# Taking |x| of softplus from ScalarE's activation to a bit mask on VectorE, and SyncE's load places from tables, in a Mamba layer with a quantised feed-forward

## Chip, cores, metric

One core of a Trainium2 chip runs the whole program. The metric is the device time of one execution in microseconds.

## What is computed

A Mamba block on a residual stream of 2 x 4096 tokens by 512, a layer norm, a feed-forward layer with weights rounded to -1, 0 or 1, and a second layer norm. The part that matters here:

```
dt = softplus(x_dbl[..., :64] @ dt_proj_w.T + dt_proj_b)        # 1024 channels
h[t] = exp(dt[t] * A) * h[t-1] + dt[t] * B[t] * x[t]              # 16 states a channel
y[t] = sum over the 16 states of h[t] * C[t]
y = (y + x * D) * silu(z);  out = y @ out_proj_w.T
```

Softplus is made as max(x, 0) + log(1 + exp(-|x|)), with a correction for the rounding of 1 + e.

## The kernel before

The Mamba part walks 16 chunks of 512 tokens (`TC`). A chunk has 64 units (`UNITS`): unit u is channel pair q = u // 16 (two blocks of 128 channels) and state n = u % 16. Each unit is a small pipeline:

- SyncE (`load_bb`, L368) brings one row of B, broadcast to 128 partitions, into a ring of four (`bb`).
- GpSimd saves the state of unit u-2 (`save_state`, L563) and makes `dbu` = `dtx` times `bb` (L592).
- ScalarE makes two `decay` tiles in PSUM (L639).
- VectorE runs two scans (L898) into one of three `h` buffers.
- TensorE transposes h (L1192, tile `ht`). ScalarE (L653) or, for twelve units, VectorE (L919) scales by C, and TensorE adds the result into y (L1197).

Everything else of the layer is placed between the units by tables written by hand, one queue for each engine, all in program order. Chunk c carries the input projection, convolution, x projection and the first half of softplus (pairs q = 0 and 1) of the next chunk f, and the output projection and norm of the one before, p. Pairs q = 2 and 3 of softplus for chunk c run at its own beginning. The first chunk's pairs 0 and 1 are made in a prologue. A loop of seven rounds with two chunks each holds chunks 1 to 14.

Softplus of a pair q is a chain across three engines, on tiles of 128x1024:

1. ScalarE takes `dt` from PSUM for each block (`take_dt`, L683, places `TAKE_DT`).
2. ScalarE: `soft` = |dt| (L690), then `soft` = exp(-soft) (L692), in places `EXP_AT`: pairs 2 and 3 in units 3 and 5, pairs 0 and 1 of f in units 48 and 50.
3. VectorE: `rounded` (L872), `dt` = max(dt, 0) + soft (L878, the lift), in places `ROUND_AT` and `LIFT_AT`; these come after the scans of units 5 and 7, and 50 and 52.
4. ScalarE: the logarithm (L698); GpSimd: the excess (L531); VectorE: the sum (L884).
5. GpSimd: `dtx` = dt times x (L539), in places `DTX_AT`.

VectorE's places count three for a unit: 3u comes ahead of its first scan, 3u+1 between the two scans, 3u+2 after both. ScalarE's and TensorE's places count two for a unit.

The weights of the input projection pass through two slots (`win`), one block of 128 columns at a time: z0, x0 to x7, z1 to z7 in a chunk. SyncE loads a block (L366) once the block before it in the same slot has been used (`wait_full`). SyncE has one queue, and a wait in it holds up the `bb` loads behind it.

Of the kernel before, what the change touches and what calls it, by code (L numbers as in the profile page):

```python
# [18 lines left out]
NB = DI // P  # L19
KM = DM // P  # L20
# [47 lines left out]
UNITS = (NB // 2) * NS  # L68
# [66 lines left out]

def banks():

    order = []
    for at in sorted(SLOTS):
        for kind, i, _ in SLOTS[at]:  # L140
            if (kind, i) not in order:
                order.append((kind, i))
    return {name: n % 2 for n, name in enumerate(order)}


BANK = banks()


# [13 lines left out]
def layer(nc, x_tm, x_cm, w_in, conv_w, conv_b, w_xp, w_dt, b_dt, a_log, d_skip, w_out, b_rows, x1, w1, b1, w2, b2, out):  # L162

    ctx = ExitStack()
    with ctx:
# [90 lines left out]
        alog_in = sem("alog_in")  # L256
        win_in = {kind: [sem(f"win_{kind}{i}") for i in range(2)] for kind in "xz"}
        xt_in = sem("xt_in")
# [99 lines left out]
        def _(sp):  # L358
# [3 lines left out]

            def load_win(kind, i):
                block_of = i + (NB if kind == "z" else 0)
                slot = (i + 1) % 2 if kind == "x" else i % 2
                sp.dma_start(win[:, slot, :, :], w_in[block_of]).then_inc(win_in[kind][i % 2], 16)  # L366

# [64 lines left out]
            for i in range(2, NB):  # L432
                wait_full(sp, "x", first, i - 2)
                load_win("x", i)
            store_b(first)

            def chunk(c, is_first, is_last):
# [4 lines left out]

                for u in range(UNITS):
                    if u == 0:
                        if is_first:
                            wait_full(sp, "x", c, NB - 1)
                        else:
                            wait_full(sp, "z", p, NB - 1)
                        load_win("z", 0)
                        if not is_last:  # L450
                            load_win("x", 0)
                        wait(sp, b_out, c, 16, 16)
                    load_bb(c, u)
                    if u == 2 and not is_last:
                        load_xt(f, tok_f)
                    if u == 4 and not is_first:
                        load_x(p, tok_p)
                    if u == 9 and not is_last:
                        wait_full(sp, "z", c, 0)
                        load_win("x", 1)  # L460
                    for i in range(2, NB):
                        if u == 22 + 2 * i and not is_last:
                            wait_full(sp, "x", f, i - 2)
                            load_win("x", i)
                    for i, at in ((1, 38), (2, 40), (3, 42), (4, 44), (5, 50), (6, 58), (7, 60)):
                        if u == at:
                            if i >= 3:
                                wait_full(sp, "z", c, i - 2)
                            elif not is_last:
                                wait_full(sp, "x", f, NB - 3 + i)  # L470
                            elif i == 2:
                                wait_full(sp, "z", c, 0)
                            load_win("z", i)
                    if u == 49 and not is_last:
# [149 lines left out]
        def _(act):  # L624
# [215 lines left out]
        def _(dve):  # L840
# [18 lines left out]
            def conv_save(f, i):  # L859
# [271 lines left out]
        def _(pe):  # L1131
            pe.wait_ge(ident_set, 1)

            def in_proj(kind, chunk, i, parts, room):
                slot = (i + 1) % 2 if kind == "x" else i % 2
                if 0 in parts:
                    room(kind, chunk, i)
                    if i == 0:
                        wait(pe, xt_in, chunk, 16, 16)
                    wait(pe, win_in[kind][i % 2], chunk, NB // 2 * 16, (i // 2 + 1) * 16)  # L1140
                for k in parts:
# [87 lines left out]

            def last_z(p):  # L1230

                held = [None, None]
                for i in (NB - 2, NB - 1):
                    held[BANK["z", i]] = ("z", p, i)
                return held
# [3 lines left out]
            for i in range(NB):  # L1239
                in_proj("x", first, i, range(KM), room)  # L1240
            pe.wait_ge(weights_in, 16 * N_WEIGHTS)
# [5 lines left out]
            def chunk(c, is_first, is_last):  # L1247
                p, f = c.near(-1), c.near(1)
                room = prologue if is_first else rooms(last_z(p))

                def slot(at):
                    for kind, i, parts in SLOTS.get(at, ()):
                        if kind == "z":
                            in_proj("z", c, i, parts, room)
                        elif kind == "o":
                            if not is_first:
                                out_proj(p, i, parts, room)
                        elif not is_last:
                            if kind == "x":
                                in_proj("x", f, i, parts, room)  # L1260
                            elif kind == "xd":
# [131 lines left out]
```

## Time and profile before

| | us |
|---|---|
| median of 3 runs | 5187.58 |
| the runs | 5177.46 to 5194.58 |
| the profiled execution | 5189.64 |
| its span in the profile | 5187.8 |
| TensorE busy | 4515.9 (87% of the span) |
| VectorE busy | 4051.2 (78%) |
| ScalarE busy | 3573.7 (69%) |
| GpSimd busy | 3165.4 (61%) |

Read the shares with care: they are means over the Mamba part, which takes about the first 4150 us, and the feed-forward part behind it, in which GpSimd does nothing and TensorE is busy nearly all the time.

### The profile page before, as it was taken

The numbers are of one execution on the slowest core, as the hardware profiler recorded it, in microseconds if no ns is written. First come the engines' busy times: TensorE is split into PE (matmuls) and PEld (weight loads), VectorE is DVE, ScalarE is ACT, GpSimd is POOL, SyncE is SP. The second block draws the span as 40 slices with busy tenths as digits, with TensorE's granted clock in tenths as the row PEclk, the third lists the DMA queues.
The fourth block names the chain that finished last, engine by engine and source line by source line (L and its number), as shares of the span: only waits on it lengthen the run. The fifth ranks groups of instructions, "written<-read, shape, count | busy, mean of one in ns | idle before, by whom it ended". The sixth has DMA issues, their size and how long they took to land.

```text
span 5187.8 us, 85358 instructions
## 1 busy us (share of the span) xinstructions
PE 4515.9 (87%) x23362; PEld 3155.1 (61%) x23362; DVE 4051.2 (78%) x4782; ACT 3573.7 (69%) x6726; POOL 3165.4 (61%) x2471
## 2 busy tenths in 40 slices
PE   5979897989797989897989898888888799999998
PEld 3656565656565656555655555555555568888887
DVE  5888888888888888888888888888888864444454
ACT  5888887878787878787878787878787722222222
POOL 4787868686868686868686868686868600000000
PEclk8999998989999989898989898999998899999999
DMA  3323323332323233333333333232324300110000
GB/s 95 97 89 96 98 93 97 92 100 91 100 90 100 93 99 90 98 90 98 90 98 91 98 91 99 92 102 89 100 90 148 109 17 33 37 43 32 32 32 33
DMA packets 233374, 436.69 MB, mean 84 GB/s; under 512 B 23968, under 2 KB 24096, under 8 KB 232416
## 3 DMA queue, kind: packets, MB, share of 16 engines
q1 hardware_dynamic: 232928, 431.55, 27.0%
q8 instruction: 181, 2.97, 0.2%
q14 instruction: 265, 2.17, 0.1%
HBM read 397.38 MB, written 34.08 MB: 83 GB/s over the span
## 4 chain that ended last, share of the span: by engine, by line
PE 58%; ACT 13%; DVE 13%; issue 10%; POOL 4%; DVEq 1%; ACTq 1%; DMA 0%; POOLq 0%; SPq 0%
PE gemm L1142 13%; PE ht L1192 12%; PE y L1197 9%; PE ht L1319 8%; DVE h L898 7%; PE gemm L1176 5%; ACT ch L653 5%; PE y L1332 4%; PE gemm L1332 4%; ACT decay L639 4%; POOL dbu L592 2%; PE gemm L1152 2%; POOL x L526 1%; ACT dt L683 1%; ACT soft L690 1%
## 5 line engine op out<-in xcount | busy, mean ns | idle before, releaser
L898 DVE TENSOR_TENSOR_SCAN h<-decay,carry,dbu 128x512 f32<-128x512 f32 x2048 | 2522.8, 1269 | 296.0 <-ACT decay L639 178.9
L592 POOL TENSOR_TENSOR dbu<-dtx,bb 128x1024 f32<-128x1024 f32 x1024 | 2458.2, 2401 | 5.6 <-issue 2.4
L639 ACT ACTIVATE decay<-dt,aneg 128x512 f32<-128x512 f32 x2048 | 1429.3, 700 | 689.0 <-DVE h L898 684.7
L1192 PE MATMUL ht<-ident,h 128*128 128x128 f32 x8192 | 1342.5, 292 | 620.5 <-DVE h L898 458.6
L1192 PEld LDWEIGHTS ht<-ident,h 128*128 128x128 f32 x8192 | 1018.6, 149 | 1335.6 <-issue 830.3
L653 ACT ACTIVATE ch<-ht,ct 128x256 f32<-128x256 f32 x3328 | 1401.3, 481 | 110.8 <-PE ht L1192 108.2
L1142 PE MATMUL gemm<-xt,win 128*128 128x512 f32 x2048 | 1063.3, 604 | 11.0 <-DMA win<-w_in 7.2
L1197 PEld LDWEIGHTS y<-ident,ch 128*128 128x128 f32 x6656 | 795.3, 144 | 404.1 <-issue 363.8
L1197 PE MATMUL y<-ident,ch 128*128 128x128 f32 x6656 | 898.5, 279 | 4.2 <-DVE x L925 2.6
L566 POOL TENSOR_TENSOR carry<-h,ones_pair 128x2 f32<-128x2 f32 x1022 | 271.4, 266 | 870.3 <-DVE h L898 860.1
L818 ACT ACTIVATE hr<-ht,b1c 128x512 f32<-128x512 f32 x256 | 176.4, 689 | 707.9 <-PE ht L1319 707.9
L1176 PE MATMUL gemm<-wout,x 128*128 128x512 f32 x1024 | 532.4, 607 | 0.0
L1099 DVE CAST hhi<-hr 128x512 fp32r<-128x512 f32 x256 | 109.4, 427 | 461.6 <-ACT hr L818 461.5
L1319 PE MATMUL ht<-xhi,wq 128*128 128x512 f32 x1024 | 398.9, 390 | 0.8 <-DVE xres L932 0.8
L1319 PE MATMUL ht<-xlo,wq 128*128 128x512 f32 x1024 | 398.8, 389 | 0.0
L1142 PEld LDWEIGHTS gemm<-xt,win 128*128 128x128 f32 x2048 | 317.3, 194 | 28.2 <-issue 20.9
L919 DVE SCALAR_TENSOR_TENSOR ya<-ht,ct,ya 128x256 f32<-128x256 f32 x512 | 221.3, 477 | 116.8 <-PE ht L1192 116.3
L855 DVE SCALAR_TENSOR_TENSOR x<-gemm,cw,x 128x511 f32<-128x511 f32 (+2 forms) x384 | 281.3, 733 | 20.6 <-ACT x L661 15.8
L1319 PEld LDWEIGHTS ht<-xhi,wq 128*128 128x128 f32 x1024 | 192.3, 188 | 42.8 <-DVE xres L932 1.6
L1319 PEld LDWEIGHTS ht<-xlo,wq 128*128 128x128 f32 x1024 | 192.2, 188 | 40.4
L1332 PE MATMUL y<-wq,hhi 128*128 128x512 f32 x512 | 204.7, 400 | 4.0 <-DVE hlo L1101 3.8
L1332 PE MATMUL gemm<-wq,hhi 128*128 128x512 f32 x512 | 200.5, 392 | 0.0
(91 smaller groups left out, 3974.8 us busy)
## 6 DMA issues: line engine op xcount, KB each, us to landing
bb<-b_rows SPq DMA_DIRECT2D x1024, 256.0 KB, 3.3
win<-w_in SPq DMA_DIRECT2D x256, 256.0 KB, 3.7
xt<-x_cm SPq DMA_DIRECT2D x16, 1024.0 KB, 6.8
xres<-x_tm SPq DMA_DIRECT2D x16, 1024.0 KB, 6.9
x<-xres SPq DMA_DIRECT2D x16, 1024.0 KB, 5.1
xr<-x SPq DMA_DIRECT2D x16, 1024.0 KB, 5.4
out<-xr SPq DMA_DIRECT2D x16, 1024.0 KB, 4.3
raw<-w SPq DMA_DIRECT2D x8, 1024.0 KB, 7.5
```

Source lines behind the costliest of these rows:

```text
L566: nc.gpsimd.tensor_tensor(carry[:, c.par, n, pair(q)], h[:, H_SLOT[u], :, TC - 1], ones[:, :], ALU.mult)\
L592: nc.gpsimd.tensor_tensor(dbu[:, u % 2, :, :], dtx[:, pair(q), :], bb[:, u % BB_RING:u % BB_RING + 1, :].to_broadcast([P, 2, TC]), ALU.mul ...
L639: nc.scalar.activation(DA[j][:, :], dt[:, c.par, i, :], ACT.Exp, scale=aneg[:, i, n:n + 1])\
L653: ins = nc.scalar.activation(ch[:, b % 2, tb, :], HT[k][:, tb % 2, :], ACT.Copy, scale=ct[:, c.par, tb, n:n + 1])
L855: nc.vector.scalar_tensor_tensor(x[:, f.par, i, back:], G[BANK["x", i]][:, 0:TC - back], cw[:, i, KC - 1 - back:KC - back], x[:, f.par, i, ...
L898: nc.vector.tensor_tensor_scan(h[:, H_SLOT[u], j, :], DA[j][:, :], dbu[:, u % 2, j, :], carry[:, c.par, n, i:i + 1], ALU.mult, ALU.add).th ...
L1142: ins = nc.tensor.matmul(G[BANK[kind, i]][:, :], win[:, slot, k, :], xt[:, chunk.par, k, :], start=(k == 0), stop=(k == KM - 1))
L1176: ins = nc.tensor.matmul(G[BANK["o", tb]][:, :], x[:, p.par, i, tb * P:(tb + 1) * P], wout[:, i, :], start=(i == 0), stop=(i == NB - 1))
L1192: ins = nc.tensor.transpose(HT[k][:, tb % 2, j * P:(j + 1) * P], h[:, H_SLOT[u], j, tb * P:(tb + 1) * P], ident[:, :])
L1197: return nc.tensor.matmul(Y[j][:, tb * P:(tb + 1) * P], src, ident[:, :], start=begins and tb == 0, stop=False, is_transpose=True, skip_gr ...
L1319: ins = nc.tensor.matmul(HP[j % 2][:, :], w1q[k][:, j * P:(j + 1) * P], part[:, k, :], start=(k == 0 and part is xhi), stop=(k == KM - 1 a ...
L1332: ins = nc.tensor.matmul(OP[tb][:, :], part[:, j % 2, tb * P:(tb + 1) * P], w2q[j // KM][:, j % KM, :], start=(j == 0 and part is hhi), st ...
```

## The change

The ScalarE activation Abs is gone. VectorE masks the sign bit instead, in places of its own: pair 2 ahead of the scans of unit 4, pair 3 ahead of those of unit 6, pair 0 of f after the scans of unit 49, and pair 1 of f between the two scans of unit 51. ScalarE's exp waits for it. Its own places are unchanged.

SyncE's loads of `win` have their places from a table: a block is loaded five units after the unit in which the block before it in its slot is last used. Places go from 26, 28, ... 36 to 24, 26, ... 34 for x2 to x7; from 38, 40, 42, 44, 50, 58, 60 to 36, 38, 40, 42, 48, 56, 58 for z1 to z7; and from 9 to 6 for x1. In a unit they now stand ahead of that unit's `bb` load and no longer behind it. The slots have one semaphore each, and TensorE's waits count on these.

```
+ABS_AT = {12: 2, 18: 3, 149: 0, 154: 1}
+XT_AT, X_AT, B_AT = 2, 4, 49
+LOAD_LAG = 5
+def loads(order):
+    at = {}
+    for n in range(len(order)):
+        if n < 2:
+            u = 0
+        else:
+            last = max(slot for slot in SLOTS for kind, i, _ in SLOTS[slot] if (kind, i) == order[n - 2])
+            u = min(last // 2 + LOAD_LAG, UNITS - 1)
+        at.setdefault(u, []).append(n)
+    return at
...
+            def load_next_win(c, order, n):
+                user = order[n - 2] if n >= 2 else WIN_ORDER[n - 2]
+                owner = c if n >= 2 else c.near(-1)
+                wait_full(sp, user[0], owner.near(1) if user[0] == "x" else owner, user[1])
+                load_win(n % 2, order[n][0], order[n][1])
...
                 for u in range(UNITS):
+                    order, at = (WIN_LAST, WIN_LAST_AT) if is_last else (WIN_ORDER, WIN_AT)
+                    for n in at.get(u, ()):
+                        if is_first and n < 2:
+                            wait_full(sp, "x", c, NB - 2 + n)
+                            load_win(n, order[n][0], order[n][1])
+                        else:
+                            load_next_win(c, order, n)
...
                     load_bb(c, u)
...
             def softplus_exp(f, q):
-                wait(act, dt_ready, f, NP, q - 1)
-                wait_read(act, "dt", f, 2 * q + 1)
-                nc.scalar.activation(soft[:, q % 2, :, :], dt[:, f.par, pair(q), :], ACT.Abs).then_inc(abs_ready, 1)
                 wait(act, abs_ready, f, NP, q + 1)
                 nc.scalar.activation(soft[:, q % 2, :, :], soft[:, q % 2, :, :], ACT.Exp, scale=-1.0).then_inc(e_ready, 1)
...
+            def softplus_abs(f, q):
+                wait(dve, dt_ready, f, NP, q - 1)
+                wait_read(dve, "dt", f, 2 * q + 1)
+                nc.vector.tensor_scalar(soft[:, q % 2, :, :].bitcast(U32), dt[:, f.par, pair(q), :].bitcast(U32), 0x7FFFFFFF,
+                                        None, ALU.bitwise_and)\
+                    .then_inc(abs_ready, 1)
...
+            for q in (0, 1):
+                softplus_abs(first, q)
...
+                    if at in ABS_AT:
+                        if ABS_AT[at] >= 2:
+                            softplus_abs(c, ABS_AT[at])
+                        elif not is_last:
+                            softplus_abs(f, ABS_AT[at])
                     for q in ROUND_AT.get(at, ()):
```

## Rows read from the trace of the kernel before

**Rows 1.** The page's chain that ended last, by engine and by line.

```profile
PE 58%; ACT 13%; DVE 13%; issue 10%; POOL 4%; DVEq 1%; ACTq 1%; DMA 0%; POOLq 0%; SPq 0%
PE gemm L1142 13%; PE ht L1192 12%; PE y L1197 9%; PE ht L1319 8%; DVE h L898 7%; PE gemm L1176 5%; ACT ch L653 5%; PE y L1332 4%; PE gemm L1332 4%; ACT decay L639 4%; POOL dbu L592 2%; PE gemm L1152 2%; POOL x L526 1%; ACT dt L683 1%; ACT soft L690 1%
```

**Rows 2.** All instructions of one line: ns as min/median/max, first and last start.

```profile
L690 ACT ACTIVATE soft<-dt x64: 1040/1094/1195, 64.0 to 3937.8; 128x1024 f32<-128x1024 f32 x64
...
L872 DVE TENSOR_SCALAR rounded<-soft x64: 667/894/2253, 67.5 to 3943.1; 128x1024 f32<-128x1024 f32 x64
```

**Rows 3.** Timeline, ScalarE, units 48 to 51: start, length, instruction, idle before.

```profile
1535.29 1.19 ACT L690 ACTIVATE soft<-dt 128x1024 f32<-128x1024 f32 x1
1536.51 1.06 ACT L692 ACTIVATE soft<-soft 128x1024 f32<-128x1024 f32 x1
...
1545.06 1.12 ACT L690 ACTIVATE soft<-dt 128x1024 f32<-128x1024 f32 x1
1546.21 1.06 ACT L692 ACTIVATE soft<-soft 128x1024 f32<-128x1024 f32 x1
```

**Rows 4.** Timeline, VectorE, the scans of units 49, 50 and 51.

```profile
1532.41 2.53 DVE L898 TENSOR_TENSOR_SCAN h<-decay,carry,dbu 128x512 f32<-128x512 f32 x2 [1.31 <-ACT decay L639]
1538.28 2.52 DVE L898 TENSOR_TENSOR_SCAN h<-decay,carry,dbu 128x512 f32<-128x512 f32 x2 [3.34 <-ACT decay L639]
...
1545.02 2.44 DVE L898 TENSOR_TENSOR_SCAN h<-decay,carry,dbu 128x512 f32<-128x512 f32 x2
```

**Rows 5.** Timeline, VectorE and then GpSimd, units 3 to 7 of a chunk.

```profile
1610.63 2.45 DVE L898 TENSOR_TENSOR_SCAN h<-decay,carry,dbu 128x512 f32<-128x512 f32 x2
...
1621.50 1.67 DVE L872 TENSOR_SCALAR rounded<-soft 128x1024 f32<-128x1024 f32 x1
1623.09 3.53 DVE L878 SCALAR_TENSOR_TENSOR dt<-dt,soft 128x1024 f32<-128x1024 f32 x1
1626.54 3.62 DVE L898 TENSOR_TENSOR_SCAN h<-decay,carry,dbu 128x512 f32<-128x512 f32 x3
...
1612.83 2.36 POOL L592 TENSOR_TENSOR dbu<-dtx,bb 128x1024 f32<-128x1024 f32 x1
...
1621.32 1.27 POOL L539 TENSOR_TENSOR dtx<-dt,x 128x512 f32<-128x512 f32 x1
...
1623.18 2.36 POOL L592 TENSOR_TENSOR dbu<-dtx,bb 128x1024 f32<-128x1024 f32 x1
```

**Rows 6.** Timeline, pair 2's Abs and sum in this chunk and the next.

```profile
1616.18 1.08 ACT L690 ACTIVATE soft<-dt 128x1024 f32<-128x1024 f32 x1
...
1653.85 3.15 DVE L884 SCALAR_TENSOR_TENSOR dt<-soft,dt 128x1024 f32<-128x1024 f32 x1
...
1877.72 1.08 ACT L690 ACTIVATE soft<-dt 128x1024 f32<-128x1024 f32 x1
...
1884.51 1.21 DVE L878 SCALAR_TENSOR_TENSOR dt<-dt,soft 128x1024 f32<-128x1024 f32 x1
1885.64 3.63 DVE L898 TENSOR_TENSOR_SCAN h<-decay,carry,dbu 128x512 f32<-128x512 f32 x3
...
1911.60 3.14 DVE L884 SCALAR_TENSOR_TENSOR dt<-soft,dt 128x1024 f32<-128x1024 f32 x1
```

**Rows 7.** Group of the lift: busy us, mean ns of one, idle us before.

```profile
L878 DVE SCALAR_TENSOR_TENSOR dt<-dt,soft 128x1024 f32<-128x1024 f32 x64 | 91.6, 1431 | 0.0
```

**Rows 8.** Busy time by stretch: PE, PEld, DVE, ACT, POOL, then granted clock, DMA.

```profile
1629.30:1632.70 3.40, 3.35 (x10) 2.21 (x11) 3.40 (x4) 3.26 (x7) 3.40 (x3) 0.50 0.03 8
```

**Rows 9.** `win` and `bb`: group, z3's last matmuls, unit 48's dbu, landing of `bb`.

```profile
L1142 PE MATMUL gemm<-xt,win 128*128 128x512 f32 x2048 | 1063.3, 604 | 11.0 <-DMA win<-w_in 7.2 <-DVE hist L863 3.8
...
1776.60 1.02 PE L1142 MATMUL gemm<-xt,win 128*128 128x512 f32 x2
...
1782.04 2.36 POOL L592 TENSOR_TENSOR dbu<-dtx,bb 128x1024 f32<-128x1024 f32 x1
...
DMA to landing us min/median/max: 3.0/3.3/7.8
```

More of the change, by code:

```diff
@@ L140, in banks @@
         for kind, i, _ in SLOTS[at]:
-            if (kind, i) not in order:
+            if kind in kinds and (kind, i) not in order:
                 order.append((kind, i))
-    return {name: n % 2 for n, name in enumerate(order)}
+    return order
+def banks():
+    return {name: n % 2 for n, name in enumerate(begun(KINDS))}
+def loads(order):
[8 more added lines that the diff above has]
+    return at
 BANK = banks()
+WIN_ORDER = begun("xz")
+WIN_LAST = begun("z")
+WIN_AT, WIN_LAST_AT = loads(WIN_ORDER), loads(WIN_LAST)
 STATS_AFTER = {1: (0, 1), 2: (2, 3)}
@@ L256, in layer @@
         alog_in = sem("alog_in")
-        win_in = {kind: [sem(f"win_{kind}{i}") for i in range(2)] for kind in "xz"}
+        win_in = [sem(f"win_in{i}") for i in range(2)]
         xt_in = sem("xt_in")
@@ L443, in chunk @@
                 for u in range(UNITS):
-                    if u == 0:
[L445 to L451, printed above, removed]
+                    order, at = (WIN_LAST, WIN_LAST_AT) if is_last else (WIN_ORDER, WIN_AT)
[5 more added lines that the diff above has]
+                            load_next_win(c, order, n)
+                    if u == 0:
                         wait(sp, b_out, c, 16, 16)
                     load_bb(c, u)
-                    if u == 2 and not is_last:
+                    if u == XT_AT and not is_last:
+                        wait_full(sp, "z", p, NB - 1)
                         load_xt(f, tok_f)
-                    if u == 4 and not is_first:
+                    if u == X_AT and not is_first:
                         load_x(p, tok_p)
[L458 to L474, printed above, removed]
+                    if u == B_AT and not is_last:
                         store_b(f)
@@ L1132, in _, with in_proj @@
             pe.wait_ge(ident_set, 1)
-            def in_proj(kind, chunk, i, parts, room):
-                slot = (i + 1) % 2 if kind == "x" else i % 2
+            def in_proj(kind, chunk, i, parts, room, n, earlier=NB // 2):
+                slot = n % 2
                 if 0 in parts:
@@ L1139, in in_proj @@
                         wait(pe, xt_in, chunk, 16, 16)
-                    wait(pe, win_in[kind][i % 2], chunk, NB // 2 * 16, (i // 2 + 1) * 16)
+                    wait(pe, win_in[slot], chunk if kind == "z" else chunk.near(-1), NB * 16, (earlier + n // 2 + 1) * 16)
                 for k in parts:
@@ L1228, in rooms, with held_after, held_at_end @@
                 return room
-            def last_z(p):
+            def held_after(p):
+                order = begun(KINDS)
                 held = [None, None]
-                for i in (NB - 2, NB - 1):
-                    held[BANK["z", i]] = ("z", p, i)
+                for kind, i in order[-2:]:
+                    held[BANK[kind, i]] = (kind, p if kind in "zo" else p.near(1), i)
+                return held
+            def held_at_end(last):
+                held = [None, None]
+                for kind, i in begun("zo"):
+                    held[BANK[kind, i]] = (kind, last if kind == "z" else last.near(-1), i)
                 return held
@@ L1239, in _ @@
             for i in range(NB):
-                in_proj("x", first, i, range(KM), room)
+                in_proj("x", first, i, range(KM), room, i, NB)
             pe.wait_ge(weights_in, 16 * N_WEIGHTS)
@@ L1248, in chunk @@
                 p, f = c.near(-1), c.near(1)
-                room = prologue if is_first else rooms(last_z(p))
+                room = prologue if is_first else rooms(held_after(p))
                 def slot(at):
@@ L1253, in slot @@
                         if kind == "z":
-                            in_proj("z", c, i, parts, room)
+                            n = (WIN_LAST if is_last else WIN_ORDER).index((kind, i))
+                            in_proj("z", c, i, parts, room, n)
                         elif kind == "o":
@@ L1259, in slot @@
                             if kind == "x":
-                                in_proj("x", f, i, parts, room)
+                                in_proj("x", f, i, parts, room, WIN_ORDER.index((kind, i)))
                             elif kind == "xd":
@@ L1289, in _ @@
             sum_over_n(last, UNITS - 1)
-            room = rooms(last_z(last))
+            room = rooms(held_at_end(last))
             room("o", last, 1)
@@ L1297, in _ @@
             transpose_rows(0, 0, 0, range(2))
-            room = rooms(last_z(last))
+            room = rooms(held_at_end(last))
             for tb in range(TB):
```

15 lines of the change are left out of this document (7 added, 8 removed).

## The prediction

> **What bounds the kernel now.** I read the chain that ended last first. TensorE holds 58% of it, ScalarE and VectorE 13% each, GpSimd 4% [rows 1]. No engine is the bound throughout: the chain changes hands inside each chunk. Abs itself (L690) has 1% of the chain, about 50 us, and its 64 instructions are only 64 x 1.09 = 70 us [rows 1, 2]. So most of Abs lies on the path today, and the question is what takes its place. For that I read the timeline at the two stretches in which it runs.
>
> Units 48 to 51 belong to ScalarE. VectorE waits 1.31 and 3.34 us for the decays of units 49 and 50 [rows 4], while ScalarE goes without a gap through dt, Abs and exp [rows 3].
>
> Units 3 to 7 belong to VectorE and GpSimd together. Each hinders the other there. The rounding of pair 2 takes 1.67 us where its fastest copy takes 0.67 [rows 5, 2]. It starts at 1621.50, GpSimd's dtx runs from 1621.32 to 1622.59, and 1622.59 + 0.6 is where the rounding ends. The lift behind it takes 3.53 us: GpSimd's dbu of unit 7 runs from 1623.18 to 1625.54, and 1.1 us later the lift is done [rows 5]. One chunk later the same lift takes 1.21 [rows 6]. So these VectorE instructions and GpSimd's exclude each other, and it is an open race which goes first. Over all 64 lifts the mean is 1.43 [rows 7], so (1.43 - 1.21) x 64 / (3.53 - 1.21) = 6 are long ones: of the 15 chunks after the first, six lose this race and nine win it. A lost race costs more than itself. From Abs of pair 2 to its sum a chunk that loses takes 1653.85 - 1616.18 = 37.7 us, one that wins 1911.60 - 1877.72 = 33.9 [rows 6]. The first scan of unit 6 is later by (1626.54 - 1616.18) - (1885.64 - 1877.72) = 2.4 us. The remaining 1.4 us is TensorE: it waits for those scans, and the stretch after it runs at a granted clock of 0.50, the lower level of 1.2 GHz [rows 8].
>
> The Trainium skill says the same of the two engines (SBUF — State Buffer, Who interferes with whom): a VectorE instruction with two SBUF inputs, or a one-input one that uses both ports, and a GpSimd instruction lock each other out for whole instructions. The trace agrees with its 1.67 and 3.53 us. The term below would be the same without this sentence.
>
> **The new instruction.** The trace has no bitwise mask. The nearest row is the rounding: also one input, one constant, 128x1024, SBUF to SBUF, 0.67 us when free [rows 2]. Slowest I allow the free lift's 1.21 us, at one element a step [rows 6]. I take 0.6 us of exclusive use, since the new instruction differs from the rounding only in operation and type.
>
> **Pairs 0 and 1 of the next chunk (15 times).** Pair 0: ScalarE is free at about 1535.3, where Abs starts today [rows 3]. VectorE ends unit 49's scans at 1532.41 + 2.53 = 1534.94 and then waits 3.34 us, so the mask fits in and ends at about 1535.6. With a wait of 0.15 the exp starts at 1535.75 instead of 1536.51 [rows 3, 4]: 0.75 us gained, up to 1.1 at best. GpSimd is held up by 0.6 at most and its next dbu is not wanted for 6 us.
> Pair 1: the mask stands after the first scan of unit 51. This starts at 1545.02, now 0.75 earlier, and ends 1.25 later at 1545.5. The mask ends at 1546.15 and exp starts at 1546.3. Before it started at 1546.21, which sounds like a draw; in the other form of this stretch, where the rounding ahead is 2.25 us (the longest of its rows [rows 2]) in place of 1.95, it comes 0.3 later, at 1546.6. Behind that exp stand the decay and the C scaling of the next units, for which TensorE waits. So pair 1 gives back all that pair 0 gained, and a little more: +0.35 us on this path, with ends of -0.75 (everything gained is kept) and +1.2 (a mask of 1.21 us). 15 x 0.35 = **+5 us**.
>
> **Pairs 2 and 3 (15 like these, and the first chunk).** Pair 2's mask is issued when unit 3's scans end, 1610.63 + 2.45 = 1613.08. GpSimd's dbu of unit 4 has the ports from 1612.83 to 1615.19 [rows 5]. The mask runs from 1615.2 to 1615.8. ScalarE gains 1.08 us on its exp, but nobody needs it: GpSimd, busy without a gap from here to 1625.5, is now 0.6 late with dtx and the dbu of units 5 and 6, and scans of unit 5 end at about 1622.0 instead of 1621.6.
> Then VectorE has rounding, lift and now the mask of pair 3 ahead of unit 6's scan; GpSimd has dtx, the saved state and unit 7's dbu. In the likelier orders one dtx (1.27) and one dbu (2.36) come ahead of the mask: even if the lift wins against the dbu, the dbu has been waiting and goes ahead of the mask. Counting from dbu of unit 6, which ends at 1621.95: 1.25 + 0.6 + 2.36 + 1.1 + 0.6 gives 1627.9 for unit 6's first scan. Before it was 1626.54 in a losing chunk, and 1624.1 would be the winning one. If the mask slips in ahead of the dbu, it is 1625.6.
> In time: a losing chunk gets 1.35 longer, a winning one 3.8 + 1.35 = 5.1. All bad: 6 x 1.35 + 9 x 5.1 = 54 us. All good: 1.5 more than a winning chunk, with part of TensorE's loss 1.8; 9 x 1.8 - 6 x (3.8 - 1.8) = +4 us. I take two chunks in three for the bad order: 0.67 x 54 + 0.33 x 4 = **+37 us**.
> ScalarE's exp of pair 3 must now wait for the mask, from 1624.7 to about 1628. Queued behind it is the decay of unit 7, but this needs the scan of unit 6 anyway.
>
> **Prologue.** VectorE is idle there, and two Abs of 1.04 us [rows 2] leave a bare chain: **-2 us**.
>
> **Load places.** Today `win` costs TensorE 7.2 us in one wait, at the very start, over 2048 matmuls [rows 9]. Earlier loads can't gain more than nothing. What they can lose: a `win` load waits for TensorE, and now `bb` loads stand behind it. The tightest place is unit 48. Its `bb` now waits until z3 has been used, 1776.60 + 1.02 = 1777.6. With one `win` issue of about 0.4 us ahead it lands 3.3 us later at 1781.4, and unit 48's dbu is to start at 1782.04 [rows 9]. If two transfers at a time slow it, by 1 us say, the dbu is 0.4 late; VectorE's 1.31 us wait for ScalarE in unit 49 covers that [rows 4]. So **0**; uncovered at the slowest landing, 7.8 us, it is 7.8 - 3.3 - 0.65 - 1.3 = 2.5 us in each such chunk. x1 to x7 have more room, as their units come later than TensorE's use. The lists of x_t and of the stored B keep their units.
>
> **Sum.** 5 + 37 - 2 = +40 us on the profiled execution: 5189.6 + 40 = 5229.6. This execution lies 2.1 above the median of the runs shown, so 5228.
>
> **The rivals.**
> - *ScalarE sets the pace (faster).* If the masks of pairs 1 and 3 were ready when ScalarE arrives, as pair 0's nearly is, the path would shrink by Abs itself. For: Abs has 1% of the chain. Against: pair 3's mask stands behind the rounding and lift of pair 2, and ScalarE comes to its exp two us before them. All four would give 15 x 4.4 = 66 us, two of four, pairs 0 and 2, 15 x (0.75 + 1.08) = 27 us, so 5160. It decides where the mask is done before ScalarE's dt is. The Trainium skill (ScalarE: Activation LUTs, Rules for kernel authors) would send simple functions to VectorE for speed alone; by the two shortest rows that is 1.04 against 0.67, and it does not count the queue. Chance 0.17.
> - *The race falls well (no change).* Shifting GpSimd by 0.6 us makes VectorE win everywhere: +4 + 5 - 2, so 5195; with pair 1 at its good end, 5185. Chance 0.13.
> - *The `bb` loads come late.* The wait at unit 48 is not covered: up to 15 x 1.5 = 22 us on top, 5250. For: 0.65 us of room. Against: the cover in unit 49. Chance 0.07.
> - *The mask goes at one element a cycle and locks nobody out.* Then pair 2 is free, pair 3 adds 1.2 x 1.3 in each chunk and pair 1 adds 1.2: 15 x 2.7 - 2 = +39. Another mechanism, same time; it is part of my forecast's 0.63.
>
> **How the numbers follow.** A measurement of this kernel tells about 0.3% (15 us) from no change. My forecast, 0.63, and late `bb`, 0.07, are slower: 0.70. Same 0.13, faster 0.17. The range goes down to 5172, which takes in the well-falling race and half of the faster case, and up to 5262, all chunks bad with 1.2 us for each pair 1. Left out are about 2 in 10.
>
> **What would show it.** Mask: L-group of 128x1024 at 0.67 us when free, with about 2.7 us for pair 2. ScalarE idle ahead of exp: about 1.5 to 2 us for pair 1, 2 to 3 for pair 3, released by VectorE. From unit 3 to the sum of pair 2: 39 us in most chunks. More stretches at half clock behind unit 6. `bb` at unit 48 landing within 1 us of its dbu. I am wrong if the mask of pair 3 goes ahead of dbu in most chunks, or if the pattern of the race elsewhere, which I did not follow past unit 13, changes with the new phase.

## The result and the profile after

| | before | after |
|---|---|---|
| median of the timed runs, us | 5189.04 (12 runs) | 5206.1 (12 runs, 5196.45 to 5212.76) |
| ratio | 1 | 1.0035, 95% interval 1.0024 to 1.0045 |
| profiled run / its span, us | 5189.6 / 5187.8 | 5212.76 / 5211.0 |

The change costs 17 us. It is slower, as forecast, but by less than half of the 40 us.

In the chain that ended last of the kernel after, ScalarE has 9% where it had 13%, VectorE 15% where it had 13%, and the issue share grew from 10% to 12% [rows 1]. Abs has left the chain; VectorE has taken part of its place.

```profile
PE 56%; DVE 15%; issue 12%; ACT 9%; POOL 5%; DVEq 1%; ACTq 0%; POOLq 0%; DMA 0%; SPq 0%
PE gemm L1171 12%; PE ht L1221 12%; DVE h L920 8%; PE y L1226 8%; PE ht L1357 8%; PE gemm L1205 5%; PE y L1370 4%; PE gemm L1370 4%; ACT ch L670 3%; ACT decay L656 3%; POOL dbu L609 3%; PE gemm L1181 2%; POOL x L543 2%; DVEq L54 1%; DVE dt L900 1%
```

All instructions of the mask's line in the kernel after, ns as min/median/max, first and last start:

```profile
L883 DVE TENSOR_SCALAR soft<-dt x64: 659/675/2980, 60.7 to 3958.0; 128x1024 uint32<-128x1024 uint32 x64
```

Its groups of the lift and of dbu, busy us, mean ns, idle us before and what ended it:

```profile
L900 DVE SCALAR_TENSOR_TENSOR dt<-dt,soft 128x1024 f32<-128x1024 f32 x64 | 90.7, 1418 | 0.0
...
L609 POOL TENSOR_TENSOR dbu<-dtx,bb 128x1024 f32<-128x1024 f32 x1024 | 2459.3, 2402 | 9.8 <-DMA bb<-b_rows 4.6
```

A free mask takes 0.66 to 0.68 us, which is the rounding's time [rows 2]. Its longest is 2.98, so it does exclude GpSimd, and GpSimd it.

Units 3 to 6 of one chunk in the timeline, VectorE and then GpSimd. This answers to [rows 5]:

```profile
859.28 2.66 DVE L883 TENSOR_SCALAR soft<-dt 128x1024 uint32<-128x1024 uint32 x1
...
865.57 2.46 DVE L920 TENSOR_TENSOR_SCAN h<-decay,carry,dbu 128x512 f32<-128x512 f32 x2 [1.27 <-POOL dbu L609]
867.95 0.67 DVE L894 TENSOR_SCALAR rounded<-soft 128x1024 f32<-128x1024 f32 x1
868.53 2.30 DVE L900 SCALAR_TENSOR_TENSOR dt<-dt,soft 128x1024 f32<-128x1024 f32 x1
870.75 0.68 DVE L883 TENSOR_SCALAR soft<-dt 128x1024 uint32<-128x1024 uint32 x1
871.36 2.45 DVE L920 TENSOR_TENSOR_SCAN h<-decay,carry,dbu 128x512 f32<-128x512 f32 x2
...
867.98 1.77 POOL L556 TENSOR_TENSOR dtx<-dt,x 128x512 f32<-128x512 f32 x1
869.72 1.17 POOL L583 TENSOR_TENSOR carry<-h,ones_pair 128x2 f32<-128x2 f32 x1
870.84 2.82 POOL L609 TENSOR_TENSOR dbu<-dtx,bb 128x1024 f32<-128x1024 f32 x1
```

Read it as a row of handovers. The rounding starts 0.03 us ahead of dtx and runs free, in 0.67. dtx waits for it (1.77 where 1.27 is its free time) and the lift waits for dtx (2.30 for 1.21). GpSimd's small copy of the state (`carry`, 0.19 when free) then waits for the lift, and while it does, the dbu behind it is not yet there to claim the ports. So the mask of pair 3 goes first, in 0.68, and the dbu waits. By "the ports" I mean, as in the prediction, what these two engines cannot use at once. In 12 of the 15 chunks ahead of the last the mask of pair 3 is free like this (14 in after_again, 13 in mask_only and in mask_pairs23). In the other three, the first among them, and in the last chunk it is blocked, as here:

```profile
1634.93 1.84 DVE L894 TENSOR_SCALAR rounded<-soft 128x1024 f32<-128x1024 f32 x1
1636.69 1.21 DVE L900 SCALAR_TENSOR_TENSOR dt<-dt,soft 128x1024 f32<-128x1024 f32 x1
1637.83 2.84 DVE L883 TENSOR_SCALAR soft<-dt 128x1024 uint32<-128x1024 uint32 x1
...
1636.17 0.65 POOL L583 TENSOR_TENSOR carry<-h,ones_pair 128x2 f32<-128x2 f32 x1
1636.78 3.33 POOL L609 TENSOR_TENSOR dbu<-dtx,bb 128x1024 f32<-128x1024 f32 x1
```

Here dtx won. The copy of the state is over as the lift begins (1636.82), the dbu queues up during the lift (1636.78), and the mask has to let it pass.

Units 49 to 51 of the kernel after, VectorE and then ScalarE, for [rows 3, 4]:

```profile
1289.41 0.67 DVE L883 TENSOR_SCALAR soft<-dt 128x1024 uint32<-128x1024 uint32 x1
1291.88 2.53 DVE L920 TENSOR_TENSOR_SCAN h<-decay,carry,dbu 128x512 f32<-128x512 f32 x2 [1.80 <-ACT decay L656]
...
1290.11 1.06 ACT L706 ACTIVATE soft<-soft 128x1024 f32<-128x1024 f32 x1
...
1300.81 1.06 ACT L706 ACTIVATE soft<-soft 128x1024 f32<-128x1024 f32 x1 [1.97 <-DVE soft L883]
```

VectorE's wait ahead of unit 50 fell from 3.34 to 1.80 us, and ScalarE now waits 1.97 us for pair 1's mask.

For the comparison by place I add up, over the 15 chunks ahead of the last, the time between the first scans of named units, as they stand in VectorE's timelines. Three profiles have Abs on ScalarE (before, before_again, loads_only), three have all four masks (after, after_again, mask_only):

| units | Abs on ScalarE | all four masks | mean difference |
|---|---|---|---|
| 0 to 3 | 157.6, 158.8, 159.7 | 162.7, 161.7, 159.1 | +2.5 |
| 3 to 6 | 216.0, 211.9, 216.6 | 222.6, 220.8, 223.4 | +7.4 |
| 6 to 13 | 437.5, 434.9, 437.5 | 433.7, 431.3, 431.4 | -4.5 |
| 13 to 40 | 1534.7, 1535.9, 1535.5 | 1535.7, 1535.6, 1535.2 | +0.1 |
| 40 to 52 | 673.0, 673.6, 673.5 | 673.4, 671.5, 672.5 | -0.9 |
| 55 to 60 | 281.3, 283.2, 282.8 | 289.2, 290.2, 289.0 | +7.0 |
| last chunk, 3 to 6 | 13.5, 13.5, 13.5 | 16.9, 16.8, 16.9 | +3.4 |

The places that I had priced are 3 to 13 and 48 to 52. Units 6 to 13 got shorter because the long lifts are gone: in the kernel before they took 30.4 us in four of the six chunks that lost the race and 29.0 or 29.1 in the others behind the first; in the kernel after 29.0, and 31.3 once. Units 55 to 60 are as dear as 3 to 6, and I had no term for them. What happens there shows in one chunk of each kernel: the window, then VectorE's two rows in it, of before and of after.

```profile
1565.01:1571.81 6.80, 3.95 (x18) 2.29 (x19) 6.53 (x9) 3.31 (x6) 5.47 (x4) 1.00 0.20 70
```

```profile
1568.47 0.88 DVE L919 SCALAR_TENSOR_TENSOR ya<-ht,ct,ya 128x256 f32<-128x256 f32 x2 [0.27 <-PE ht L1192]
1569.26 1.27 DVE L898 TENSOR_TENSOR_SCAN h<-decay,carry,dbu 128x512 f32<-128x512 f32 x1
```

```profile
1577.02:1583.82 6.80, 5.38 (x12) 2.67 (x12) 4.92 (x8) 2.07 (x3) 4.83 (x3) 0.51 0.17 39
```

```profile
1582.20 0.88 DVE L941 SCALAR_TENSOR_TENSOR ya<-ht,ct,ya 128x256 f32<-128x256 f32 x2 [1.68 <-PE ht L1221]
1583.00 1.27 DVE L920 TENSOR_TENSOR_SCAN h<-decay,carry,dbu 128x512 f32<-128x512 f32 x1
```

The columns of a window are busy time and instructions of PE, PEld, DVE, ACT and POOL, then granted clock, DMA share and GB/s. TensorE's 18 matmuls of the first window take 0.22 us on average, the 12 of the second 0.45. At the same place after unit 54's first scan the granted clock is 1.00 in the one and 0.51 in the other, 2.4 GHz and 1.2. In the second TensorE's transposes come later, VectorE's product with C waits 1.68 us for them instead of 0.27, and so the second scan of unit 56 starts 1.7 us later. By the start of unit 57 1.1 us of it is left. In all six profiles this holds chunk by chunk: behind the first chunk, unit 57 starts 17.7 us after unit 54 where the clock is full in this stretch and 18.8 where it is halved throughout; most chunks lie between, in clock and in time. Full were 8, 4 and 5 of the 15 chunks with Abs on ScalarE, and 1, 0 and 0 with the masks.

### The profile page after: what moved, and what is told of

It is laid out like the page before. It is cut to its first block, busy times and chain, and to the rows that moved or that the text cites. A ratio compares the mean times of both kernels' runs of the same rounds, so it can differ in the third digit from the quotient of the medians.

```text
span 5211.0 us, 85386 instructions
## 1 busy us (share of the span) xinstructions
PE 4538.0 (87%) x23362; PEld 3163.9 (61%) x23362; DVE 4106.5 (79%) x4846; ACT 3515.1 (67%) x6662; POOL 3189.4 (61%) x2471
## 4 chain that ended last, share of the span: by engine, by line
PE 56%; DVE 15%; issue 12%; ACT 9%; POOL 5%; DVEq 1%; ACTq 0%; POOLq 0%; DMA 0%; SPq 0%
PE gemm L1171 12%; PE ht L1221 12%; DVE h L920 8%; PE y L1226 8%; PE ht L1357 8%; PE gemm L1205 5%; PE y L1370 4%; PE gemm L1370 4%; ACT ch L670 3%; ACT decay L656 3%; POOL dbu L609 3%; PE gemm L1181 2%; POOL x L543 2%; DVEq L54 1%; DVE dt L900 1%
## 5 line engine op out<-in xcount | busy, mean ns | idle before, releaser
L1171 PE MATMUL gemm<-xt,win 128*128 128x512 f32 x2048 | 1077.1, 611 | 11.9 <-DMA win<-w_in 7.3
L583 POOL TENSOR_TENSOR carry<-h,ones_pair 128x2 f32<-128x2 f32 x1022 | 282.9, 277 | 857.7 <-DVE h L920 847.1
```

What stands on the lines that cost most here:

```text
L583: nc.gpsimd.tensor_tensor(carry[:, c.par, n, pair(q)], h[:, H_SLOT[u], :, TC - 1], ones[:, :], ALU.mult)\
L1171: ins = nc.tensor.matmul(G[BANK[kind, i]][:, :], win[:, slot, k, :], xt[:, chunk.par, k, :], start=(k == 0), stop=(k == KM - 1))
```

## The experiments

Their times stand beside those of the kernel before on the same chip. loads_only, mask_only, mask_pairs01 and mask_pairs23 shared one chip (before 5188.24 us); mask_pair2, mask_pair3, after_dtx8 and mask01_early another (5194.31); mask23_at12, mask012, mask012_early and before_again a third (5188.98); mask_pair2_again, mask02 and after_again a fourth (5183.67).

**Only one half of the change.** loads_only: the new load tables, Abs left on ScalarE. mask_only: the masks, the old load places.

```
 # loads_only, softplus_exp
+                wait(act, dt_ready, f, NP, q - 1)
+                wait_read(act, "dt", f, 2 * q + 1)
+                nc.scalar.activation(soft[...], dt[...], ACT.Abs).then_inc(abs_ready, 1)
```

> The changed kernel with Abs back on ScalarE, so only the load places differ from the kernel before. Theory A: within 3 us of the kernel before. Theory B: +12 to +17 us, with GpSimd waiting for bb at unit 48. Theory C: no loss in units 3 to 13 or 40 to 52, but a different count of half-clock stretches in units 0 to 3 and 55 to 60, and up to 10 us either way.

> The kernel before with the mask on VectorE in its four places, SyncE's loads as before. Theory A (the mask, by its place ahead of the scans of unit 6 and by the shared lock, makes the loss): the whole loss stays, +15 to +20 us against the kernel before. Theory B (the load places make it, by bb loads held up at unit 48 and by win loads at other times): 0 to +5 us. Theory C (the loss is in stretches at half clock that any small shift of the chunks moves about): a result between -10 and +20 us that does not add up with the loads-only kernel to +17.

loads_only: 5185.94 us, ratio 0.9996 (0.9986 to 1.0006). mask_only: 5205.17, 1.0037 (1.0023 to 1.0052). The whole loss is the mask's; the load places cost nothing. In the kernel after GpSimd did wait for `bb`, 4.6 us in seven waits (group of dbu above), 1.0 at most; by these two runs it costs nothing.

**Half of the pairs.** mask_pairs01 masks pairs 0 and 1 on VectorE and leaves Abs of 2 and 3 on ScalarE; mask_pairs23 is the reverse.

```
-ABS_AT = {12: 2, 18: 3, 149: 0, 154: 1}
+ABS_AT = {149: 0, 154: 1}     # mask_pairs01; mask_pairs23: {12: 2, 18: 3}
```

> The changed kernel with pairs 2 and 3 back on ScalarE's Abs; pairs 0 and 1 are masked on VectorE in places 149 and 154. From the profile of the changed kernel these two come out even (ScalarE wins 0.9 us at the exp of pair 0 and waits 1.97 us for the mask of pair 1). Theory A: 0 +- 4 us against the kernel before, since pairs 2 and 3 carry the loss. Theory C: the units 40 to 52 even, and the total wherever the half-clock stretches fall.

> The changed kernel with pairs 0 and 1 back on ScalarE's Abs; pairs 2 and 3 are masked in places 12 and 18. Theory A: +13 to +20 us, all of the loss. The stretch of units 3 to 6 should take 14.4 us in most chunks, as in the changed kernel, and 17 in those where dbu goes ahead. Theory C: units 3 to 13 give no more than +3 us over all chunks, and the rest of any loss lies in units 0 to 3 and 55 to 60.

mask_pairs01: 5190.21 us, 1.0004 (0.9994 to 1.0014). mask_pairs23: 5206.67, 1.0039 (1.0026 to 1.0053), 18 us. The loss lies with pairs 2 and 3. But it does not lie at one place. Against the mean of the three profiles with Abs on ScalarE, mask_pairs23 takes 4.4 us more in units 3 to 6, 4.2 less in 6 to 13, 3.4 more in the last chunk's 3 to 6, 1.6 more in 55 to 60, and 8.4 more in units 0 to 3, where the kernel after has only 2.5.

**Pair 2 alone and pair 3 alone.**

```
-ABS_AT = {12: 2, 18: 3, 149: 0, 154: 1}
+ABS_AT = {12: 2}              # mask_pair2; mask_pair3: {18: 3}
```

> The changed kernel with only pair 2 masked on VectorE (place 12); the other three on ScalarE. Theory A1 (the 0.6 us of pair 3's mask, in VectorE's queue ahead of unit 6's scans, is the loss): within 4 us of the kernel before; units 3 to 6 take 13.5 or less in most chunks. Theory A2 (pair 2's mask waits 2 us for GpSimd and then holds GpSimd up by 0.6 us, in a stretch where GpSimd has no gap): +5 to +12 us, and units 3 to 6 take 14 us.

> The changed kernel with only pair 3 masked on VectorE (place 18). Theory A1: +10 to +17 us, units 3 to 6 at 14 to 14.5 us in chunks where 13.5 was the short form. Theory A2: +3 to +8 us. If neither alone costs more than 5 us, it is the two together that do.

mask_pair2: 5171.43 us, 0.9954 (0.9941 to 0.9967), 23 us faster (12 in the repeat on another chip, below). mask_pair3: 5228.26, 1.0066 (1.0053 to 1.0079), 34 us slower. Of one instruction, at two places of one stretch, one gains and the other loses. Units 3 to 6 add up to 206.9 and 245.4 us, where 212 to 217 is usual. Units 0 to 3 move too, without a mask in them: 150.0 and 141.7 us for 157.6 to 159.7. So the loss of pair 3's mask in units 3 to 13, 35 us, is larger than what the whole profiled execution lost (5219.79 us, the fastest of five, 25 over before). Pair 3 alone, VectorE and then GpSimd:

```profile
867.86 1.56 DVE L898 TENSOR_SCALAR rounded<-soft 128x1024 f32<-128x1024 f32 x1
869.33 1.21 DVE L904 SCALAR_TENSOR_TENSOR dt<-dt,soft 128x1024 f32<-128x1024 f32 x1
870.47 2.84 DVE L887 TENSOR_SCALAR soft<-dt 128x1024 uint32<-128x1024 uint32 x1
873.23 1.27 DVE L924 TENSOR_TENSOR_SCAN h<-decay,carry,dbu 128x512 f32<-128x512 f32 x1
...
867.57 1.28 POOL L556 TENSOR_TENSOR dtx<-dt,x 128x512 f32<-128x512 f32 x1
...
869.42 3.34 POOL L609 TENSOR_TENSOR dbu<-dtx,bb 128x1024 f32<-128x1024 f32 x1
```

This is the order that I had forecast: dtx first, then the dbu that has waited through the lift, then the mask. Unit 3 to unit 6 takes 16.2 us where a winning chunk of before takes 13.5, in 7 of the 15 chunks; seven more take 16.5 to 16.8, five of them with the dbu ahead of the lift instead. Pair 2 alone (VectorE, then ScalarE's Abs of pair 3):

```profile
855.84 0.67 DVE L898 TENSOR_SCALAR rounded<-soft 128x1024 f32<-128x1024 f32 x1
856.42 2.30 DVE L904 SCALAR_TENSOR_TENSOR dt<-dt,soft 128x1024 f32<-128x1024 f32 x1
858.64 3.76 DVE L924 TENSOR_TENSOR_SCAN h<-decay,carry,dbu 128x512 f32<-128x512 f32 x3
...
857.45 1.07 ACT L708 ACTIVATE soft<-dt 128x1024 f32<-128x1024 f32 x1
```

Pair 2's mask holds dtx back: it now starts 11.05 us after unit 3's first scan instead of 10.6, and the rounding at 11.0 instead of 10.9. So the rounding wins in 13 of 15 chunks, the lift takes 2.30 there, and unit 6 comes at 13.8 us after unit 3, 14.3 at most. The margin is thin: the two start within 0.03 us of each other, and in one chunk of mask_pairs23 dtx won from the same start times. The lost races of before, 15.9 to 16.2 us in six chunks, are gone.

**dtx out of the way.** after_dtx8 is the kernel after with dtx of block 3 in unit 8 instead of 6, so that the lift of pair 2 need not wait for it.

```
-DTX_AT = {60: (0,), 61: (1,), 4: (2,), 6: (3,), ...}
+DTX_AT = {60: (0,), 61: (1,), 4: (2,), 8: (3,), ...}
```

> The changed kernel with one more edit: GpSimd makes dtx block 3 in unit 8 and not in unit 6, so that its 1.27 us are no longer between VectorE's rounding and its lift. Lock theory (the two exclude each other): the lift of pair 2 falls from 2.30 to 1.2 us, units 3 to 6 from 14.4 to about 13.2, and the time by 10 to 18 us against the changed kernel, to about 5190. If the lift is 2.3 us for a reason of its own, nothing changes.

5230.92 us, 1.0067 (1.0054 to 1.0080): 37 us slower than before, so about 20 slower than after, where I expected a gain. VectorE and then GpSimd:

```profile
865.47 0.67 DVE L894 TENSOR_SCALAR rounded<-soft 128x1024 f32<-128x1024 f32 x1
866.05 1.22 DVE L900 SCALAR_TENSOR_TENSOR dt<-dt,soft 128x1024 f32<-128x1024 f32 x1
867.18 2.84 DVE L883 TENSOR_SCALAR soft<-dt 128x1024 uint32<-128x1024 uint32 x1
...
875.49 2.29 DVE L900 SCALAR_TENSOR_TENSOR dt<-dt,soft 128x1024 f32<-128x1024 f32 x1
...
866.14 3.34 POOL L609 TENSOR_TENSOR dbu<-dtx,bb 128x1024 f32<-128x1024 f32 x1
...
874.97 1.73 POOL L556 TENSOR_TENSOR dtx<-dt,x 128x512 f32<-128x512 f32 x1
```

The lift fell to 1.22 us, as meant. But without dtx the dbu is there during the lift, and the mask waits for it in all 15 chunks: 15.5 us from unit 3 to unit 6, where after has 14.4. And dtx has met the next lift, of pair 3 (2.29): against the mean of the three profiles with all four masks, units 6 to 13 take 18 us more and units 3 to 6 10 more, while 0 to 3 and 55 to 60 take 14 less. So the run's time is no clean price of the blocked mask, but the order in the rows is: dtx was what kept the dbu away from the mask.

**Pair 3's mask behind pair 2's.** mask23_at12 keeps all four masks and moves pair 3's ahead of the rounding.

```
-ABS_AT = {12: 2, 18: 3, 149: 0, 154: 1}
+ABS_AT = {12: (2, 3), 149: (0,), 154: (1,)}
```

> The kernel after with pair 3's mask moved from place 18 (behind pair 2's lift, ahead of unit 6's scans) to place 12, right behind pair 2's mask; all four masks stay on VectorE. Theory A (pair 3's mask costs by its place: behind the lift it costs 0.67 us where it keeps the shared port and 2.84 where the state update of GpSimd goes ahead): behind pair 2's mask, which has let GpSimd's waiting operation go ahead of it, it costs about 0.67 us, and unit 5's scans and the round start as much later; units 3 to 6 take 13.8 + 0.7 = 14.5 us, as after, but without the 17.0 us chunks; about 0 to -8 us against the kernel after, so 1.002 to 1.0035. Rival B: the second mask in a row waits for GpSimd as pair 1's did at place 150 (2.8 us); then units 3 to 6 take 15.5 to 16 us and the time is about 1.006 to 1.008.

5194.3 us, 1.0005 (0.9994 to 1.0017): no difference from before, where after has 1.0035. VectorE (both masks in one row), then GpSimd:

```profile
853.36 4.35 DVE L883 TENSOR_SCALAR soft<-dt 128x1024 uint32<-128x1024 uint32 x2
...
855.42 1.74 POOL L556 TENSOR_TENSOR dtx<-dt,x 128x512 f32<-128x512 f32 x1
```

The second mask waits, but for the shorter dtx, and takes 1.77 us in most chunks. This delays unit 4 (6.6 us behind unit 3 instead of 4.9), and the next two units follow sooner (2.5 and 5.3 us instead of 3.7 and 5.8), so that the usual chunk takes 14.4 as before the move. What is gone are the chunks of 17: units 3 to 6 sum up to 216.0 us, and the last chunk takes 14.5 instead of 16.9. Both of my prices were off: it is neither 0.67 for the mask nor 2.8. Units 55 to 60 kept their loss (290.1).

**Pair 1 early.** mask01_early has pairs 0 and 1 masked and pair 1's mask right behind pair 0's.

```
-ABS_AT = {12: 2, 18: 3, 149: 0, 154: 1}
+ABS_AT = {149: 0, 150: 1}
```

> Masks for pairs 0 and 1 only, pair 1's moved from place 154 to 150, ahead of the scans of unit 50, where VectorE waits 1.8 us anyway; pairs 2 and 3 on ScalarE. If ScalarE sets the pace in units 48 to 51, as the 1.97 us of its wait for pair 1's mask say, units 48 to 55 get 1.9 us shorter in each of 15 chunks: 28 us, about 5160. If another engine takes over at once (GpSimd or VectorE), half of that or less.

5187.68 us, 0.9982 (0.9971 to 0.9992), 7 us where I had expected 28. VectorE, then GpSimd:

```profile
1031.40 3.57 DVE L887 TENSOR_SCALAR soft<-dt 128x1024 uint32<-128x1024 uint32 x2
1034.90 2.45 DVE L924 TENSOR_TENSOR_SCAN h<-decay,carry,dbu 128x512 f32<-128x512 f32 x2
...
1032.08 2.35 POOL L609 TENSOR_TENSOR dbu<-dtx,bb 128x1024 f32<-128x1024 f32 x1
```

The two masks take 3.57 us, since the dbu goes between them. The scan of unit 50 comes no earlier than before. Units 40 to 52 gain 5 us against before and 52 to 55 3.5, and 55 to 60 lose 3 to 5 again.

**Combinations.** mask012 has pairs 0, 1 and 2 masked (149, 154, 12), mask012_early the same with pair 1 at 150, mask02 pairs 0 and 2 (149, 12). The other pairs have Abs on ScalarE. mask_pair2_again and after_again are repeats, before_again is the kernel before.

> The kernel after with pair 3's absolute value alone back on ScalarE (activation in front of its Exp); pairs 0, 1 and 2 are masked on VectorE at places 149, 154 and 12. Theory A (the loss is pair 3's mask behind pair 2's lift, pair 2's mask gains, and the effects add up): pair 2's mask alone gave 0.9954 and pairs 0 and 1 alone 1.0004, so about 0.9958 of the kernel before, or about -22 us; units 3 to 6 take 13.8 to 13.9 us a chunk where they took 14.4 to 14.6 after. Rival B (the masks cost by their number, 0.67 to 2.8 us each in VectorE's queue, and pair 2's gain was of that run's own): with three of four masks about 1.000 to 1.002.

> As mask012, but pair 1's mask at place 150 in place of 154, right behind pair 0's. Theory A (additive): the early place of pairs 0 and 1 alone gave 0.9982 against 1.0004 for the late one, so about 0.9936, or -33 us, 11 us less than mask012, and 0.8 us less a chunk in units 48 to 52. Rival B: what the early place saves is given back in the units behind, where in the earlier profile 9 of 13 us came back; then the same as mask012 within 5 us.

> The kernel before, unchanged, profiled once more, to see how far one profile differs from another. Theory A (the stretches of units 0 to 3 and 55 to 60, and which chunks have the long lift of pair 2, differ from profile to profile with the granted clock): units 55 to 60 sum up to 1.5 to 5 us more or less than in the first profile over 15 chunks, units 0 to 3 to as much, and another number of chunks than six has units 3 to 6 at 15.9 to 16.2 us. Rival B (the same program always falls the same way): the sums agree within 1 us, and the same six chunks are long.

> Only pair 2 masked on VectorE at place 12, the kernel of mask_pair2 once more. Theory A (its gain is real, and pairs 0 and 1 cost it 10 to 15 us through units 0 to 3, since mask012 was 1.6 us at a per-chunk gain short of it): 0.995 to 0.9965 again, units 0 to 3 near 150 us over 15 chunks where mask012 had 165.6. Rival B (the gain was partly that run's own; the effects do add up): 0.998, as mask012, and units 0 to 3 at 158 to 166 us.

> Pairs 0 and 2 masked on VectorE at places 149 and 12; pairs 1 and 3 have their activation back on ScalarE. Theory A (pair 1's mask at place 154 moves units 0 to 3 and takes pair 2's gain away): as mask_pair2, 0.995 to 0.9965. Rival B (pair 0's mask, which leads unit 50 by 1 us, is the one that moves the later stretches; or the difference lies between runs): 0.998 to 0.999, as mask012.

> The changed kernel, unchanged. Theory A (the loss of 17 us is pair 3's mask in units 3 to 6, about 8 us over the 15 chunks, the last chunk's units 3 to 6, 3 to 4 us, and units 55 to 60, 6 to 8 us, which follow the granted clock at a place that the masks move systematically): about 1.0035 again; the masks of pair 3 take 0.68 us in 11 to 14 of 15 chunks; units 55 to 60 sum up to 287 to 290 us where three profiles of streams as before gave 281 to 283. Rival B (the 8 us of units 55 to 60 were that profile's chance): 281 to 284 us there.

| kernel | us | ratio (95%) | units 48 to 52, sum | units 0 to 3, sum |
|---|---|---|---|---|
| mask012 | 5183.27 | 0.9984 (0.9971 to 0.9996) | 288.1 | 165.6 |
| mask012_early | 5176.69 | 0.9975 (0.9965 to 0.9985) | 282.3 | 162.1 |
| mask_pair2_again | 5172.1 | 0.9985 (0.9976 to 0.9994) | 289.9 | 148.9 |
| mask02 | 5170.96 | 0.9967 (0.9955 to 0.9978) | 274.2 | 161.3 |
| after_again | 5204.64 | 1.0043 (1.0029 to 1.0057) | 287.1 | 161.7 |
| before_again | 5190.95, one run | | 291.1 | 158.8 |

The effects don't add up: pairs 0, 1 and 2 together are 6 us faster than before, not 22. That was not chance. mask_pair2 came out at 5171.4 and 5172.1 on two chips (the ratios differ by 0.3% because before did, 5194 and 5184, so its gain is 12 to 23 us), and its units 0 to 3 sum up to 150.0 and 148.9 us, where the three combinations that also mask pair 0 have 161 to 166. The difference is in a few chunks of 13 us and more in units 0 to 3, where the others take about 9: one in either profile of pair 2 alone, none with pair 3 alone, four or five in the combinations. Counted from 0 they are chunks 3, 7, 9 and 11 in before, before_again, after and mask02 alike, each the first of a round of the loop. In all of these TensorE's weight loads stand still for 4.2 to 5.7 us in units 1 and 2 and wait for nothing that the profile shows; in the other chunks from 1 to 14 such a standstill is 2.0 us at most. The granted clock does not tell them apart: in before, chunk 3 takes 13.9 us at 0.77, chunk 4 takes 9.1 at 0.78. What the standstill is, and why the masks switch it, no run here shows. Before_again shows what one profile hides: four long chunks in units 3 to 6 instead of six, units 55 to 60 1.9 us more.

mask02 separates pair 0 from pair 1. VectorE, then ScalarE:

```profile
1027.02 0.67 DVE L887 TENSOR_SCALAR soft<-dt 128x1024 uint32<-128x1024 uint32 x1
1029.49 2.52 DVE L924 TENSOR_TENSOR_SCAN h<-decay,carry,dbu 128x512 f32<-128x512 f32 x2 [1.80 <-ACT decay L656]
...
1039.18 2.52 DVE L924 TENSOR_TENSOR_SCAN h<-decay,carry,dbu 128x512 f32<-128x512 f32 x2 [0.51 <-ACT decay L656]
...
1036.26 1.13 ACT L708 ACTIVATE soft<-dt 128x1024 f32<-128x1024 f32 x1
1037.42 1.06 ACT L710 ACTIVATE soft<-soft 128x1024 f32<-128x1024 f32 x1
```

From unit 50's first scan to unit 52's it is 9.7 us here. In the kernel after it is 10.7 in this chunk, 10.5 on average: its exp of pair 1 starts 8.9 us behind the scan of unit 50, waiting for VectorE, against 7.9 here, with an Abs in front of it. So pair 0's mask gains 1.1 us a chunk (291 to 274) and pair 1's gives 0.85 back (units 50 to 52, 145.4 to 158.1 us over the 15 chunks). mask02 has the lowest median of all, 13 us under before; pair 2 alone is 1 us away. Four of mask02's twelve executions took 5152 to 5161 us and the others 5168 to 5173, which is not explained. Against pair 2 alone, pair 0's 16 us return as 12 us in units 0 to 3 and 3 in 55 to 60.

## Why the prediction was wrong

**The failed step is the term for pairs 2 and 3: "I take two chunks in three for the bad order", +37 us.** Measured by itself (mask_pairs23) it is +18. At the place that the term is about, it is less still: units 3 to 13 and the last chunk's 3 to 6 add up to 7.4 - 4.5 + 3.4 = +6 us in the kernel after. The chunks fell the other way: the mask of pair 3 went ahead of the dbu in 12 of 15. I had named this myself as what would make me wrong. My prices for one chunk were better than the weight, but too high as well. From unit 3 to unit 6 the good order takes 14.4 us, 0.9 more than a winning chunk of before (I had 1.5), and the bad order 17.0 (I had 17.3). The 1.4 us that a lost race costs behind unit 6 are 0.6 to 0.9 on average in the three profiles with Abs on ScalarE. "All bad", which I had at 54 us, is what mask_pair3 comes nearest to (without pair 2's mask): 35 us in units 3 to 13.

With the weight as it fell, my own prices give 0.2 x 54 + 0.8 x 4 = 14 for this term and 14 + 5 - 2 = 17 in all, which is the measured loss. That would have been luck: 7 of the 17 us lie in units 55 to 60, for which I had no term.

What I missed is the link between my own two steps. I worked out that pair 2's mask makes GpSimd's dtx 0.6 us late, and then took the race behind it as if it were still as open as before. It is hardly open: a dtx 0.45 us later loses to the rounding, if only by a few hundredths of a us, the lift then holds up the state copy, and with it the dbu that would have stood in front of the mask. mask_pair2 (rounding ahead in 13 of 15 chunks) and mask_pair3 (race lost, mask blocked) show both halves, and after_dtx8 shows that dtx is the piece between.

- **The cost of a mask**, 0.6 to 0.67 us of exclusive use and about 2.7 for pair 2's: right (0.67; 2.64 to 2.78 in 11 of 15 chunks, free in three).
- **Pairs 0 and 1, +5 us**: +2 (1.0004), inside the interval. The mechanism holds, one gains what the other gives back: 0.98 us a chunk from unit 49 to 50 (I had 0.75) against 0.85 from 50 to 52 (I had 1.1). The wait of ScalarE for pair 1 was forecast at 1.5 to 2 us and is 1.97; pair 3's, forecast at 2 to 3, is 1.78 in most chunks and 4.03 in a bad one.
- **Load places, 0**: right, 0.9996. The waits for `bb` came, at most 1.0 us, and were covered.
- **Prologue, -2 us**: not to be told. The first scan starts at 83.7 to 87.7 us in the profiles with Abs on ScalarE and at 84.0 to 85.4 with all masks.
- **More half clock behind unit 6**: there the sum even falls by 4.5 us. It came in units 55 to 60, +7 us, in three profiles of three of the masks in their places; that the pattern might change where I did not follow it I had named too. That it goes with the granted clock is shown chunk by chunk; why the masks turn it there is not settled. Masks of 0, 1 and 2 leave it at 285.2, mask_pairs01 has 286.9, mask_pairs23 284.0, and all four with dtx elsewhere (after_dtx8) 284.5. The lowest is mask012_early, 281.3; mask02 has 287.5, and the other kernel with all four, mask23_at12, 290.1.
- **The last chunk**: +3.4 us that I counted as another ordinary one. There dtx goes first and the mask takes 2.98.
- **Two sums were wrong.** The race that falls well with pair 1 at its good end is 4 - 11 - 2, so 5178 and not 5185; all bad with 1.2 us for each pair 1 is 54 + 18 - 2, so 5258 and not 5262. Neither changes the forecast.
- Sum of the means in the table: 2.5 + 7.4 - 4.5 + 0.1 - 0.9 + 7.0 + 3.4 = +15 us, against +17 timed.

Of the rivals, "the race falls well" is the one that took place, with its own price too low (it foresaw 5195): the 0.67 us of pair 3's mask remains on the path, and units 55 to 60 come on top. "ScalarE sets the pace" is true of pair 0, and pair 1 gave it away. It is not true of pair 2: with its mask alone the usual chunk takes 13.8 us from unit 3 to 6, 0.3 more than a winning chunk of before, and the gain comes from the lost races that are gone and from units 0 to 3 (8, 5 and 9 us less in units 3 to 6, 6 to 13 and 0 to 3). I had written 27 us for pairs 0 and 2, and mask02, which is just these two, gains 13.

The Trainium skill (SBUF — State Buffer, Who interferes with whom) says that the order of issue, not the form of the operation, decides who is blocked. The traces agree: the same mask takes 0.67, 1.77 or 2.84 us, by what GpSimd had issued when it arrived.

## What to carry to other kernels

When an operation moves to an engine that shares a port with another, its price is set by what the other engine has waiting when it arrives. Follow each delay that the first moved operation causes into the next race, before giving that race odds. And test moved operations one by one: the four masks here are worth about -16 and +13 us (pairs 0 and 1, by units 48 to 52) and -12 to -23 and +34 us (pairs 2 and 3, each run alone). They do not add up either, since each also moves stretches that hold no mask; only the sum looked like a small loss.

## What the runs showed of the hardware

- A waiting GpSimd instruction takes the ports when VectorE's ends, even if VectorE's next one is ready: mask 2.84 us behind a lift, in mask_pair3 and after_dtx8. VectorE likewise gets its turn after one GpSimd instruction: in mask23_at12 the second mask runs behind dtx (1.77 us), and the copy of the state that GpSimd has ready waits for it (0.64 us instead of 0.19).
- The scans, of the same size per instruction as dtx but with one of their two large inputs (`decay`) in PSUM, exclude nobody: 1.25 to 1.29 us each in the whole profile, with a dbu of 2.36 beside them. A 128x2 copy on GpSimd does wait for the ports, 1.17 us instead of 0.19.
- The bitwise mask on uint32 has the same free time as the f32 rounding, 0.67 us for 128x1024.
- A granted clock of 0.51 instead of 1.00 in one 6.8 us stretch goes with 1.1 us more from unit 54 to 57, and which chunks have it differs between two profiles of the same kernel (8 chunks at full clock there in before, 4 in before_again).
- TensorE's weight loads can stand still for 4.2 to 5.7 us and wait for nothing that the profile shows: chunks 3, 7, 9 and 11 of before, before_again, after and mask02.
